# Loads on two queues, edge keys made inside the first norm, weight halving moved to GpSimd, in a graph-convolution and LSTM kernel

## The reference, cut to what matters

```python
def layernorm(x): return (x - mean) / sqrt(var + 1e-5)
h = layernorm(x) @ weight + bias                       # first norm, 256 x 256
agg = segment_sum(h[src], dst) / max(degree, 1)
x = x + agg
z = layernorm(x)                                       # second norm
xi, xf, xg, xo = z @ U_i + b_i, ..., z @ U_o + b_o
for t in range(3125):                                  # batch of 1: one state of 256
    i, f, o = sigmoid(x?_t + h @ V_?);  g = tanh(xg_t + h @ V_c)
    c = h * c + i * g                                  # f is not used
    h = o * tanh(c)
out = x + hs
```

## Time and profile before

| | |
|---|---|
| median of 3 runs | 594.93 us (594.37 to 595.94) |
| the profiled execution | 593.6 us; span from first to last instruction 591.8 us |
| busy share of the span | PE 74%, weight load 64%, DVE 70%, ACT 61%, POOL 38% |
| chain that ended last | PE 45%, DVE 31%, ACT 11%, issue 6%, SP's queue 3%, DMA 1%, POOL 1% |
| granted clock of PE, mean | 0.914 |

### The profile page before, as it was taken

How to read it: one execution, slowest core, us unless ns; L and a number is a source line. 1 busy time by engine, 2 the same in 40 slices (tenths; PEclk the granted TensorE clock), 3 DMA queues, 4 the chain that set the end, 5 groups by cost and what they waited for, 6 DMA issues and landing times.

```text
span 591.8 us, 16043 instructions
## 1 busy us (share of the span) xinstructions
PE 439.5 (74%) x6285; PEld 379.8 (64%) x6285; DVE 411.3 (70%) x1151; ACT 362.0 (61%) x976; POOL 224.0 (38%) x537
## 2 busy tenths in 40 slices
PE   1019882887998999999999996545677777777760
PEld 1007661776887889888988985444667666666650
DVE  0295769977966777786877752277777777777872
ACT  0025651454656768677777852488788888777750
POOL 5113000034334435555454523022466555555530
PEclk9998895798999999999999998655799999999995
DMA  7431003300000010000001001000000000011102
GB/s 185 141 111 44 2 16 103 100 2 1 17 30 1 1 45 3 1 24 22 2 1 45 2 1 45 1 1 2 3 3 3 4 2 3 4 45 47 35 17 89
DMA packets 17321, 17.81 MB, mean 30 GB/s; under 512 B 2294, under 2 KB 16889, under 8 KB 17239
## 3 DMA queue, kind: packets, MB, share of 16 engines
q1 hardware_dynamic: 12935, 13.03, 6.8%
q10 hardware_dynamic: 2864, 1.97, 1.3%
q0 software_dynamic: 1440, 1.71, 1.1%
HBM read 7.08 MB, written 9.61 MB: 28 GB/s over the span
## 4 chain that ended last, share of the span: by engine, by line
PE 45%; DVE 31%; ACT 11%; issue 6%; SPq 3%; DMA 1%; POOL 1%; DVEq 0%; ACTq 0%
PE bank L971 10%; PE bank L943 9%; PE bank L945 9%; DVE c_st L1503 7%; DVE ig L1497 6%; DVE h L1508 5%; ACT tc L818 5%; PE bank L1005 4%; PE bank L932 4%; SPq L447 3%; PE bank L1050 3%; DVE h_flat L1508 3%; ACT gx L711 3%; DVE hots L1434 2%; PE bank L988 2%
## 5 line engine op out<-in xcount | busy, mean ns | idle before, releaser
L1050 PE MATMUL bank<-h,V 128*128 128x63 f16 (+1 forms) x3336 | 130.7, 197 | 55.6 <-DVE h L1508 51.8
L943 PE MATMUL bank<-h_flat,counts 125*128 125x257 f16 x625 | 171.6, 277 | 0.0
L945 PE MATMUL bank<-h_flat,counts 125*128 125x256 f16 x625 | 169.7, 274 | 0.0
L1050 PEld LDWEIGHTS bank<-h,V 128*128 128x128 f16 x3336 | 117.3, 100 | 70.6 <-issue 44.5
L752 ACT ACTIVATE counts<-bank 125x500 f16<-125x500 f32 (+1 forms) x175 | 97.2, 556 | 95.2 <-PE bank L1005 93.9
L1005 PE MATMUL bank<-hots 128*128 128x125 f16 x625 | 137.1, 226 | 17.6 <-DVE hots L1434 17.6
L1434 DVE TENSOR_TENSOR hots<-iota,kp 128x1024 f16<-128x1024 f16 x157 | 104.9, 698 | 0.1
L1005 PEld LDWEIGHTS bank<-hots 128*128 128x128 f16 x625 | 60.7, 99 | 29.2 <-DVE far_f L1377 12.5
L548 POOL TENSOR_TENSOR newton<-rstd 125x1 f32<-125x1 f32 x75 | 27.2, 363 | 116.0 <-DVE rstd L1394 105.1
L971 PE MATMUL bank<-z2T,U 128*128 128x250 f16 (+1 forms) x540 | 60.5, 264 | 13.3 <-ACT gx L711 7.3
L575 POOL TENSOR_TENSOR h<-h_flat,h 128x126 f16<-128x126 f32 x82 | 41.7, 508 | 67.3 <-DVE h_flat L1508 67.3
(11 more groups left out here) (149 smaller groups left out, 636.0 us busy)
## 6 DMA issues: line engine op xcount, KB each, us to landing
h_dram<-h_flat SPq DMA_DIRECT2D x1, 3137.2 KB
x_sb<-in_x_dram SPq DMA_DIRECT2D x25, 125.0 KB
x_dram<-x_sb SPq DMA_DIRECT2D x5, 625.0 KB
out_dram<-x_sb SPq DMA_DIRECT2D x20, 125.0 KB
out_dram<-x_sb SPq DMA_DIRECT2D x5, 75.0 KB
gx<-in_L_gnn_weight_dram ACTq DMA_DIRECT2D x1, 256.0 KB, 4.7
gx<-in_L_ffn_U_i_dram ACTq DMA_DIRECT2D x1, 256.0 KB, 7.1
gx<-in_L_ffn_V_i_dram ACTq DMA_DIRECT2D x1, 256.0 KB, 7.5
```

The costliest lines, as they stand in the source:

```text
L943: nc.tensor.matmul(ps_sum[turn % 2][:, 0:D + 1], counts[:, turn % 2, s, :], line[:, s, D:2 * D + 1], start=(s == 0), stop=False, skip_grou ...
L945: return nc.tensor.matmul(ps_sum[turn % 2][:, 0:D], counts[:, turn % 2, s, :], line[:, s, 0:D], start=False, stop=(s == BLOCKS - 1), skip_ ...
L1050: mm = nc.tensor.matmul(to[:, (m - m0) * n:(m - m0 + 1) * n], V16[:, v_part, d, m * P:(m + 1) * P], h16[:, h_part, d, c0:c1], start=False, ...
```

## The change

It does six things:

1. **Loads on two queues.** For the first four chunks of x (`X_SHARED`) three of five transfers go on SP's queue and two on ACT's; the last chunk is all on SP's. U, V and the gate biases move from ACT's queue to SP's, behind x.
2. **Extremes by magnitude.** `extreme` reduces the absolute value, so that one reduction takes the place of two and `largest` loses an instruction. That of the graph weight runs ahead of the window rows, and POOL's reduction for it stands ahead of POOL's requests for window rows.
3. **Window starts** sum while they compare, and stand in block 5 of the first norm, where they stood in block 1. Statistics run 8 blocks ahead; deviations are made in the last three blocks of each chunk.
4. **Keys ahead of their transposition.** POOL converts the edges. DVE computes part and key from the edges as they lie, partition by window, in blocks 18 to 24 of the first norm (`floors`, `edge_places`). PE transposes part and key, and ACT copies them into `kp` in six pieces.
5. **Halving on POOL**, after the conversion.
6. **The work on U and V moves forward**: extremes at windows 12 and 18 of block 0, `largest` at 20, `scales` at (1, 20). PE waits for the last `line` only ahead of the first sum.

```diff
@@ SP
-                for r in range(RUN):
+                for r in range(3 if c < X_SHARED else RUN):
                     sp.dma_start(x_sb[parts(r), js, :], x_rows[c, r, :, :, :]).then_inc(x_in[c], 16)
+            for n, (U, V, b) in enumerate(((U_i, V_i, b_i), (U_c, V_c, b_c), (U_o, V_o, b_o))):
+                sp.dma_start(U_sb[:, :, n, :], U.rearrange("(a p) h -> p a h", p=P)).then_inc(weights_in, 16)
+                sp.dma_start(V_sb[:, :, n, :], V.rearrange("(a p) h -> p a h", p=P)).then_inc(weights_in, 16)
+                with nc.allow_non_contiguous_dma("bias columns"):
+                    sp.dma_start(gb[:, n, :], b.rearrange("(a p) -> p a", p=P)).then_inc(weights_in, 16)
@@ POOL
+            weights_top(1, 0, 1)
             pool.wait_ge(rows_known, 1)
...
-            weights_top(1, 0, 1)
             pool.wait_ge(starts_known, 1)
...
+            for in_ in win_edges_in:
+                pool.wait_ge(in_, 16)
+            nc.gpsimd.tensor_copy(win_edges_f, win_edges.rearrange("p b e a -> p a b e")).then_inc(edges_f, 1)
+            def halve(w, by):
+                nc.gpsimd.tensor_scalar(w, w, by, None, ALU.mult).then_inc(halved, 1)
+                weights_seq[0] += 1
+            pool.wait_ge(weights_in, 16 * 9)
+            for n in (0, 2):
+                halve(U_sb[:, :, n, :], 0.5)
+                halve(gb[:, n, :], 0.5)
+                halve(V_sb[:, :, n, :], 0.25)
+            halve(V_sb[:, :, 1, :], 0.5)
@@ ACT
+            for c in range(X_SHARED):
+                for r in range(3, RUN):
+                    act.dma_start(x_sb[r:NB:RUN, c * X_CHUNK:(c + 1) * X_CHUNK, :], x_rows[c, r, :, :, :]
+                                  ).then_inc(x_in[c], 16)
...
+            act.wait_ge(edges_ps, 1)
+            full = EDGES_FIRST * WIN_ROWS // HOT_WINDOWS
+            rest = WIN_ROWS // HOT_WINDOWS
+            for a in (PART, KEY):
+                nc.scalar.activation(kp[:, 0:full, a, :], bank[2 + a][:, 0:full * HOT_WINDOWS].rearrange(
+                    "p (k g) -> p k g", g=HOT_WINDOWS), ACT.Copy).then_inc(keys_ready, 1)
+                last_ps = edges_at(a, EDGES_FIRST)
+                nc.scalar.activation(kp[:, full:full + rest, a, :], last_ps[:, 0:rest * HOT_WINDOWS].rearrange(
+                    "p (k g) -> p k g", g=HOT_WINDOWS), ACT.Copy).then_inc(keys_ready, 1)
+                nc.scalar.activation(kp[:, full + rest, a, 0:1], last_ps[:, rest * HOT_WINDOWS:WIN_ROWS], ACT.Copy
+                                     ).then_inc(keys_ready, 1)
@@ PE
-            pe.wait_ge(edges_f, 1)
-            for a in range(2):
+            pe.wait_ge(edges_placed, 2)
+            for a, of in ((PART, edge_part), (KEY, edge_key)):
                 for b in range(WIN_BATCHES):
-                    mm = nc.tensor.transpose(edges_at(a, b), win_edges_f[:, a, b, :], ident[0:WIN_ROWS, 0:WIN_ROWS])
+                    mm = nc.tensor.transpose(edges_at(a, b), of[:, b, :], ident[0:WIN_ROWS, 0:WIN_ROWS])
...
-            pe.wait_ge(keys_ready, 1)
-            pe.wait_ge(line_ready, BLOCKS)
+            pe.wait_ge(keys_ready, 6)
...
+                            if t == 0:
+                                pe.wait_ge(line_ready, BLOCKS)
@@ DVE
+            def extreme(n, w):
+                counted_op(nc.vector.tensor_reduce(w_max[:, n:n + 1], w, AX_X, ALU.max, apply_absolute_value=True))
+            dve.wait_ge(w_in, 32)
+            extreme(0, w_sb)
+            largest(0, 1)
             dve.wait_ge(before_ps, 1)
...
-                    counted_op(nc.vector.tensor_scalar(win_rows_f[:, b, :], win_rows[:, b, :], col_thr[:, b:b + 1],
-                                                       None, ALU.is_lt))
+                    counted_op(nc.vector.scalar_tensor_tensor(
+                        out=win_rows_f[:, b, :], in0=win_rows[:, b, :], scalar=col_thr[:, b:b + 1],
+                        in1=ones[0:WIN_ROWS, 0:1].to_broadcast([WIN_ROWS, EDGE_COLS]), op0=ALU.is_lt, op1=ALU.mult,
+                        accum_out=in_row[:, b:b + 1]))
                 settle()
-                link(nc.vector.tensor_reduce(in_row, win_rows_f, AX_X, ALU.add))
...
+            def floors(k):
+                if k == 0:
+                    dve.wait_ge(edges_f, 1)
+                of, by = ((win_edges_f[:, 1, :, :], RUN), (edge_run, RUN), (edge_chunk, ROWS))[k]
+                floor_of((edge_run, edge_chunk, edge_k)[k], of, by)
+            for j in range(X_CHUNK):
+                chunk_stats(j)
+            chunk_to_root(0)
             scales(0, 1, 6, 1)
+            for j in range(X_CHUNK, 2 * X_CHUNK):
+                chunk_stats(j)
             for k in range(6):
                 chunk_deviation(0, k)
+            chunk_to_root(1)
+            AHEAD = 8
+            for j in range(BLOCKS + 4):
+                c, k = divmod(j, X_CHUNK)
+                if c + 1 < BLOCKS // X_CHUNK and 2 <= k:
+                    chunk_deviation(c + 1, 2 * (k - 2))
...
+                if j == 5:
+                    window_starts()
...
+                if FLOORS_FROM <= j < FLOORS_FROM + 3:
+                    floors(j - FLOORS_FROM)
+                if FLOORS_FROM + 3 <= j < FLOORS_FROM + 7:
+                    edge_places(j - FLOORS_FROM - 3)
+            nc.vector.memset(far_f[:, :], 0.0)
+            dve.wait_ge(keys_ready, 6)
...
-            weights_work = {(0, 15): halve,
-                            (1, 0): lambda: extreme(w_max, 1, flat(U_sb), ALU.max),
-                            (1, 8): lambda: extreme(w_min, 1, flat(U_sb), ALU.min),
-                            (1, 16): lambda: extreme(w_max, 2, flat(V_sb), ALU.max),
-                            (2, 0): lambda: extreme(w_min, 2, flat(V_sb), ALU.min),
-                            (2, 4): lambda: largest(1, 3),
-                            (2, 23): lambda: scales(1, 3, 13, 2),
-                            (3, 7): lambda: x_scales(),
+            def uv_extreme(n, w):
+                if n == 1:
+                    dve.wait_ge(halved, 7)
+                extreme(n, w[:, :, :, :].rearrange("p d n h -> p (d n h)"))
+
+            weights_work = {(0, 12): lambda: uv_extreme(1, U_sb),
+                            (0, 18): lambda: uv_extreme(2, V_sb),
+                            (0, 20): lambda: largest(1, 3),
+                            (1, 20): lambda: scales(1, 3, 13, 2),
+                            (2, 7): lambda: x_scales(),
                             (5, 20): count_covered}
```

More of the change, by code:

```diff
@@ L116, in bass_gnn_lstm_kernel @@
         at[0] = 2 * RUN * MT * CHUNKS
[L117 to L121, removed]
+        edge_run, edge_chunk, edge_k, edge_part, edge_key = (
+            early(WIN_ROWS, WIN_BATCHES * WIN_EDGES).rearrange("p (b e) -> p b e", b=WIN_BATCHES) for _ in range(5))
         inside = early(P, KEYS_WIDE)
@@ L514, in _, with weights_top @@
             nc.gpsimd.memset(line[:, :, 2 * D:LINE], 1.0).then_inc(consts, 1)
+            def weights_top(n, n0, n1):
+                pool.wait_ge(w_max_ready, n)
+                nc.gpsimd.partition_all_reduce(w_top[:, n0:n1], w_max[:, n0:n1], P, bass.bass_isa.ReduceOp.max
+                                               ).then_inc(w_max_all, 1)
+            weights_top(1, 0, 1)
             pool.wait_ge(rows_known, 1)
@@ L652, in _ @@
                 act.dma_start(w_sb[:, DH * D:(DH + 1) * D], b_gnn.partition_broadcast(P)).then_inc(w_in, 16)
[L653 to L657, removed]
+            x_rows = x.rearrange("(k i s r) d -> k r i s d", k=RUN, i=ROWS, r=RUN)
+            for c in range(X_SHARED):
+                for r in range(3, RUN):
+                    act.dma_start(x_sb[r:NB:RUN, c * X_CHUNK:(c + 1) * X_CHUNK, :], x_rows[c, r, :, :, :]
+                                  ).then_inc(x_in[c], 16)
             sqrts = [0]
@@ L1287, in split_bias @@
                                                in1=b_parts[:, 0, :], op0=ALU.mult, op1=ALU.add).then_inc(b_split, 1)
-            for c in range(2):
-                for j in range(c * X_CHUNK, (c + 1) * X_CHUNK):
-                    chunk_stats(j)
-                chunk_to_root(c)
-            dve.wait_ge(w_in, 32)
-            for to, op in ((w_max, ALU.max), (w_min, ALU.min)):
-                extreme(to, 0, w_sb, op)
-            largest(0, 1)
             def window_starts():
@@ new lines, in edge_places @@
+            def edge_places(k):
+                if k == 0:
+                    link(nc.vector.scalar_tensor_tensor(out=edge_part, in0=edge_run, scalar=-float(RUN),
+                                                        in1=win_edges_f[:, 1, :, :], op0=ALU.mult, op1=ALU.add))
+                    link(nc.vector.scalar_tensor_tensor(out=edge_part, in0=edge_chunk, scalar=float(RUN),
+                                                        in1=edge_part, op0=ALU.mult, op1=ALU.add))
+                elif k == 1:
+                    nc.vector.scalar_tensor_tensor(out=edge_part, in0=edge_k, scalar=-float(RUN * ROWS), in1=edge_part,
```

(12 more changed lines are left out.)

116 lines of the change are left out of this document (34 added, 82 removed).

## The result

| | before | after |
|---|---|---|
| median of 4 runs | 594.65 us (592.76 to 595.94) | 577.73 us (574.88 to 581.94) |
| profiled execution | 593.6 us, span 591.8 | 575.94 us, span 574.1 |
| mean granted clock of PE | 0.914 | 0.917 |

The ratio is 0.9724, with a 95% interval of 0.9651 to 0.9796: 12 to 21 us faster. The two profiled executions differ by 17.66 us, and all of that lies ahead of the fourth finished block of the counting stage: DVE finishes block 3 at 148.64 before and 130.99 after (17.65), block 24 at 359.32 and 341.70 (17.62). From there the two run alike.

A forecast was written before the change was run, and what follows sets the result against it. Ahead of 142 us DVE's work was taken to bound the kernel, after slow loads. Gains of 14.6 us up to the first count and 5.5 in counting made 20.1 off 593.6, 573.5; with 1.3 for the median 574.8, range 567 to 584.

The forecast's parts named there:

- chunk 1's arrival: Loads at the start: chunk 1 of x there at 20 instead of 27.9 us, a gain of 8 us (2 to 12).
- chunk 1 to first product: Start of the first norm: the path from chunk 1 to the first product falls from 16.0 to 8.0 us, gaining 8.
- first 16 blocks: First norm: window starts in block 5 cost 3 us, and more blocks at PE's slow pace cost 1 us.
- floors and places, last 8 pitches: End of the first norm: keys' work on DVE in blocks 18 to 24 takes 15.8 us against 8.8, costing 7.
- tail, from the last product's start: After the norm loop: 13.4 us before the first count shrink to 3.8, a gain of 9.6 us.
- first count: Sum of the loop's terms: the first count moves from 98.4 to about 84 us, a gain of 14.6.
- counting stage: Early counting: POOL's 3.7 us hole taken whole plus a third of 5.4 us of DVE work, gaining 5.5 (1 to 9).
- rival B: Loads: the two queues add nearly fully, chunk 1 at 15.6 or sooner, 4.5 to 8 us more gained, about 569; chance 0.12.
- Three together do no better: Loads: claim that three DMA queues together move no more than one queue alone, which stands at 5.4 of 16 engines.
- Rival A: Loads: x arrives hardly earlier, chunk 1 at 25 or 26, 6 us less gained, 581; chance 0.16.
- Rival C: Counting stage: gives nothing because PE at half clock sets its pace, 5.5 us less gained, 580; chance 0.12.
- Rival D: Block 0 of counting: POOL's halvings come late, DVE waits in window 12, the whole slower than before; chance 0.04.

The follow-up runs named there:

- experiment 3: The version after with all of x on SP's queue, and POOL asking for window rows before its first reduction: 576.98 us, ratio 0.9691.
- experiment 5: The version after with 130 unread matmuls on PE ahead of its first transposition: 577.42 us, ratio 0.9701.
- experiment 6: On experiment 4, unread matmuls on PE: 55 ahead, 14 in the wait for block 0, 2 for each of blocks 2 to 10: 565.82 us, ratio 0.9521.
- experiment 2: The kernel before with only U, V and the gate biases moved to SP's queue behind x: 588.74 us, ratio 0.9912.
- experiment 4: The version after with each 25-partition transfer of x cut into 16 and 9 partitions: 568.75 us, ratio 0.9567.
- experiment 8: The version after with the halvings of U and V back on DVE, in window 11 of block 0: 579.98 us, ratio 0.9737.
- experiment 7: On experiment 6, 18 more unread matmuls behind the edges' transpositions and three in every fourth window: 565.94 us, ratio 0.9517.

## Why the prediction was right, and where its terms were off

574.8 us was forecast with a range of 567 to 584; the median is 577.73. By profiled executions the sum was 20.1 us and 17.66 came.

| term | predicted | measured |
|---|---|---|
| chunk 1's arrival | 8 | 27.93 - 21.39 = 6.5 |
| chunk 1 to first product | 8 | 16.02 - 7.97 = 8.0 |
| first 16 blocks (window starts -3, slow pace -1) | -4 | 30.24 - 36.17 = -5.9 |
| floors and places, last 8 pitches | -7 | 9.72 - 15.97 = -6.3 |
| tail, from the last product's start | 9.6 | 14.49 - 4.68 = 9.8 |
| first count | 14.6 | 98.40 - 86.18 = 12.2 |
| counting stage | 5.5 | 17.6 - 12.2 = 5.4 |

**Arrival.** The mechanism was right: two queues share 120 GB/s in halves (rival B, that they add, is out: 17.1% and 17.0% of the engines where one alone has 33.9%). Chunk 1 came 1.4 late (21.39 against 20). POOL's window rows went out at 12.86 and not from 17.3: I had put POOL's 7.75 us behind the reduction, and the wait lay ahead of it (12.24, after 7.52 us of "issue"). By the Trainium skill (GPSIMD Engine Reference, "Instruction dispatch") the first call of a freshly loaded library kernel costs about 6 us; read so, it belongs ahead of the reduction, and the trace agrees in the place, with 7.52. The rows then lay on SP's last transfers of chunk 1: SP moved 175 packets from 15 to 18 us and 83 from 18 to 21, by this estimate a loss of 1.6 us. But 1.5 had been put in for that; what the other 1.3 of the delay behind 18.5 is, no run shows. That asking later "moves POOL's traffic off chunk 1" holds only by halves: experiment 3 shows, with one queue, that asking still earlier costs four more. "Three together do no better" was misread: from 18 to 21 us the three queues move 0.66 MB on 71% of the engines; it is SP's and ACT's together that stay at 34%. Rival A (chunk 1 at 25 or 26) did not come.

**First blocks.** Window starts cost 5 x 0.58 and short ones, 3.6 us of DVE, yet the two pitches that hold them are only 1.5 above the slow pitch, where before has a stall of 1.1 in the same place; I had -3. What I had at -1, further blocks at the slow pace, cost most of the 5.9: nine of the first 16 pitches are 2.15 to 2.29, where before has five of 2.01 to 2.29 and most others at 1.26. This is the mis-sized term. Experiments 5 and 6 show that it is the clock and that it falls behind gaps inside the norm. That a norm which starts earlier takes longer also shows in experiment 2 (5.2 us earlier at its start, 0.9 at its end), but not in experiment 4 (7.3 earlier at its start than after, 9.6 at the first count), and why is open. Which blocks these are varies between kernels with the same code there (31.9 in experiment 8, 36.2 after), and the spread of after's runs, 574.88 to 581.94, is as wide; its median lies 1.8 above its profiled execution. That the paces make that spread was not tried.

**Keys.** The scalings of the floors (0.49 each, 0.52 with the wait) and the places of 0.81 to 0.83 as costed; ACT's copies and the tail within 0.3.

**Counting.** The 5.5 came, but not composed as I had it. Up to the first finished block the gain is 18.25 - 16.02 = 2.2 us, and none of it lies ahead of the first sum: there the second extreme took the place of the halvings, as I had it, and experiment 8 shows what it would cost with both (1.9). Behind the first sum three extremes stood before and none stands now, so that DVE has 10.40 us of work there before and 5.71 now. But PE is busy throughout in both, and by the estimate of experiment 7 its half clock, 5.4 us before and 2.0 now, makes 1.7 of the 2.3 us. The rest is DVE's: before, PE's 50th sum matmul ends at 115.89 and DVE comes to it at 116.65. Why the clock rises sooner is open. The rest of the 5.4 us, 3.2, comes between blocks 0 and 3, in after and experiment 8 alike. Of it 2.2 is the hole ahead of the first z: from the finished sum to z it takes 109.33 - 102.20 = 7.1 us instead of 9.4. DVE's wait there was 3.70 and is still 2.01, now for POOL's arithmetic and not for its start, so the 3.7 did not go whole. Rival C (PE's clock sets the pace, nothing gained) is out, since 5.4 were gained; its mechanism holds only behind the first sum, where PE is the bound and where its clock makes part of the gain. Rival D did not come: halvings done at 63.3 (I had 65), DVE asks at 87.76.

## What to carry to other kernels

Before a second queue is given to a load, look at the busy share of the engines while one queue works alone: at 34% it was the transfers' shape that bound, and cutting 25 partitions into 16 and 9 gave 9 us where the second queue gave nothing. A load's arrival is also set by what else is asked for in those microseconds: order the requests by when they are needed. Price an earlier start of a PE stage with its clock: here blocks fed with gaps ran at half clock, and the first 16 of them took back 5.9 of the 14.6 us gained at the first product. And where work leaves an engine, look at which engine is busy throughout on each side of the next hand-over: 4.7 us of DVE's work left behind the first sum, where PE was busy throughout, and 2.3 us came, 1.7 of them by the estimate from PE's clock.

## What was not expected of the hardware

- Two queues with the same shape of transfer split 120 GB/s evenly (123 and 122 packets in 2 us), and POOL's indirect transfers take x down to a third (333 to 106 packets in 3 us, beside 110 and 366 of POOL's).
- The same reduction on POOL takes 0.38, 0.69, 0.72 or 3.70 us. Where it takes 0.38, 5.6 to 7.5 us of "issue" stand ahead of it, except before and in experiment 2, where POOL waits 15.63 and 10.02 us for DVE there; where it takes 0.69 or 0.72, the next instruction starts some 7 us behind it. At 3.70 nothing stands ahead, and whether something stands behind can't be read, since the next work is asked for only 8 us later. Why it differs was not tried.
- PE's granted clock went to 0.50 by 31 us, after 17 us of unbroken work up to 25.4 and a stretch half idle (experiment 5). In the kernel after the record reads 1.00 in the same blocks while six matmuls take the same 1.54 us: a granted clock of 1.00 does not say that PE runs at the fast pace, the duration of its matmuls does.
